# First attention of a two-layer mixture kernel: chunk ends and output gates move from GpSimd to VectorE, and five batch steps in place of six stand beside the scatter of rows

## The reference

```python
# gated linear attention, 4 heads, DK 128, DV 32, chunks of 64 tokens
gk = jax.nn.log_sigmoid(x @ Wgk1 @ Wgk2 + bgk2) / 16
G = jnp.cumsum(gc, axis=-2)                      # within a chunk
qg, k_intra = qc * jnp.exp(G) * scale, kc * jnp.exp(-G)
g_last = jnp.exp(G[..., -1, :])                  # the chunk ends
def step(S, inp):                                # over the 4 chunks
    o = oi_ + jnp.einsum('bhck,bhkv->bhcv', qg_, S)
    S = S * gl_[..., :, None] + jnp.einsum('bhck,bhcv->bhkv', kg_, v_)
o = o * jax.lax.rsqrt(jnp.mean(o * o, -1) + EPS) * gnw
o = o * (g * jax.nn.sigmoid(g))                  # the output gates
s = o @ Wo
# beside it, from the same normed x: 8 experts, each token to 2 of them
g = silu(experts(xn)); x = x + s * g
```

## Time and profile before

| | us |
|---|---|
| median of 3 runs | 1236.32 |
| the three runs | 1230.03, 1236.32, 1247.06 |
| the profiled execution: time | 1231.64 |
| the profiled execution: span of the core | 1229.8 |
| its mean granted clock of TensorE | 0.816 of full speed |
| busy PE, PEld, DVE, ACT, POOL | 870.0, 652.9, 657.1, 632.8, 442.0 |

### The profile page before, as it was taken

One profiled execution on the slowest core, in us unless ns is written; L12 is line 12 of the kernel. 1 busy time (PEld: TensorE's weight loads), 2 busy tenths in 40 slices (PEclk: granted clock), 3 DMA queues, 4 the chain that ended last, 5 costly groups with the idle time before them and its releaser, 6 DMA issues.

```text
span 1229.8 us, 23628 instructions
## 1 busy us (share of the span) xinstructions
PE 870.0 (71%) x8916; PEld 652.9 (53%) x8916; DVE 657.1 (53%) x1132; ACT 632.8 (51%) x1102; POOL 442.0 (36%) x470
## 2 busy tenths in 40 slices
PE   5644777989898986078883204989999999998510
PEld 4432566878787865054551002556766766666410
DVE  7762445655555422677567002766676566763345
ACT  5442346565756431444441002668788678886522
POOL 3077351213232345000002772003454445454535
PEclk9866768988899998575796556989999899998755
DMA  9411111010101121600001311120111011110052
GB/s 326 164 54 54 42 48 29 19 28 27 28 28 28 39 59 33 157 0 1 1 1 38 134 52 35 53 70 19 36 32 32 27 36 32 32 36 19 16 147 68
DMA packets 62366, 63.92 MB, mean 52 GB/s; under 512 B 7378, under 2 KB 52322, under 8 KB 62132
## 3 DMA queue, kind: packets, MB, share of 16 engines
q1 hardware_dynamic: 53300, 43.99, 12.2%
q0 software_dynamic: 8960, 18.43, 4.6%
HBM read 31.84 MB, written 30.55 MB: 51 GB/s over the span
## 4 chain that ended last, share of the span: by engine, by line
PE 41%; ACT 18%; issue 13%; DVE 13%; another core or an unknown queue 9%; POOL 3%; DMA 2%; SPq 0%; POOLq 0%; ACTq 0%; DVEq 0%
PE bank L427 5%; PE bank L642 4%; ACT L790 4%; PE bank L579 3%; PE bank L581 3%; POOL ys L1701 2%; PE bank L593 2%; PE bank L580 2%; ACT arena L1097 2%; PE bank L695 2%; PE bank L707 2%; PE bank L668 2%; PE bank L455 2%; PE bank L688 1%
## 5 line engine op out<-in xcount | busy, mean ns | idle before, releaser
L1701 POOL DMA_INDIRECT ys<-arena x152 | 151.9, 999 | 188.2 <-DVE arena L1450 84.8
L1097 ACT ACTIVATE arena<-bank 128x512 f32<-128x512 f32 x192 | 101.7, 596 | 109.0 <-remote 67.5
L1685 POOL DMA_INDIRECT xs<-arena x128 | 128.6, 1005 | 76.9 <-DVE arena L1291 39.3
L1571 DVE TENSOR_REDUCE arena<-bank 128x2 bf16<-128x512 f32 (+1 forms) x192 | 119.8, 681 | 61.3 <-remote 43.6
L579 PE MATMUL bank<-arena 128*128 128x128 bf16 x608 | 135.2, 230 | 10.9 <-DVE arena L1431 10.0
L581 PE MATMUL bank<-arena 128*128 128x128 bf16 x608 | 134.9, 230 | 0.0
L580 PE MATMUL bank<-arena 128*128 128x128 bf16 x608 | 132.3, 225 | 0.8 <-issue 0.7
L790 ACT ACT_TABLE_LOAD x71 | 91.1, 1283 | 1.2
L427 PE MATMUL bank<-arena 128*128 128x256 f32 x256 | 70.9, 438 | 19.7 <-DVE arena L1337 17.7
L1741 POOL TENSOR_TENSOR arena<-arena 128x1024 f32<-128x1024 f32 x20 | 46.9, 2343 | 94.3 <-ACT arena L1007 94.3
L1440 DVE SCALAR_TENSOR_TENSOR arena<-arena,bank 128x512 f32<-128x512 f32 x36 | 24.8, 689 | 97.4 <-ACT arena L969 80.4
(11 more groups left out here) (212 smaller groups left out, 2106.8 us busy)
## 6 DMA issues: line engine op xcount, KB each, us to landing
xs<-arena SPq DMA_DIRECT2D x19, 516.0 KB, 9.1
arena<-xs SPq DMA_DIRECT2D x38, 258.0 KB, 2.8
arena<-ys SPq DMA_DIRECT2D x32, 256.0 KB, 5.3
arena<-in_MF SPq DMA_DIRECT2D x8, 512.0 KB
ys<-arena POOLq DMA_INDIRECT x152
arena<-in_x SPq DMA_DIRECT2D x8, 256.0 KB, 5.5
arena<-in_W SPq DMA_DIRECT2D x8, 256.0 KB
xs<-arena POOLq DMA_INDIRECT x128
```

The costliest lines, as they stand in the source:

```text
L1097: act(PT[kt_][:, i, gs[0]:gs[0] + len(gs), :], bank_of["s2", b, n, i][:, :].rearrange("p (g q) -> p g q", q=w), ACT.Exp, scale=8 ** -0.5). ...
L1571: red(negM[b % 2][:, u, 32 * i + gs[0]:32 * i + gs[0] + len(gs)], kv_, op=ALU.max, negate=True).then_inc(m_max.sem, 1)
L1685: eng.indirect_dma_start(xs[l][:, :], bass.IndirectOffsetOnAxis(ap=slot_i[l][:, m:m + 1], axis=0), xrow[:, t, :], None).then_inc(rows_move ...
L1701: eng.indirect_dma_start(ys[l][:, :], bass.IndirectOffsetOnAxis(ap=yid[g % 4][:, j:j + 1], axis=0), y[:, 128 * j:128 * j + 128], None).the ...
```

## The change

The two pieces leave GpSimd's list and stand in VectorE's: the copy of the chunk ends in `scaled`, just before the first bank of queries is scaled, and the product with the gates in `gated`, just before the two multiplies that use it. The semaphores stay the same. The scatter is cut in fifths, each ahead of one of the attention's steps 1 to 5; the pieces of W1 are dealt out anew; step 6 and all that follow stand beside groups of experts, 14 steps beside groups 0 to 13.

```diff
-OUTPUTS_EARLY = 7
+OUTPUTS_EARLY = 6
@@ walk
-            for t in range(1, 7):
-                do["scatter"](0, t - 1, 6)
+            for t in range(1, 6):
+                do["scatter"](0, t - 1, 5)
                 if t == 1:
                     do["set_later"]()
                 for part in range(3):
                     do["gla"](t, part)
-                for c in range(8 * (t - 1) // 6, 8 * t // 6):
+                for c in range(8 * (t - 1) // 5, 8 * t // 5):
                     do["w1"](c)
             do["ffn0_begin"]()
             for g in range(19):
                 for part in range(3):
                     do["ffn0"](g, part)
-                    if 7 + g < 20:
-                        do["gla"](7 + g, part)
+                    if 6 + g < 20:
+                        do["gla"](6 + g, part)
@@ vector
+            def chunk_ends(b):
+                P5 = bufP.rearrange("p (h n i) -> p n h i", h=4, n=4)
+                if b >= 4:
+                    eng.wait_ge(*state.at(b - 4))
+                cp(ends[b % 4], P5[:, 0:3, :, 63:64].rearrange("p n h o -> p n (h o)")).then_inc(p_ends.sem, 1)
+
             def scaled(b):
                     eng.wait_ge(*qk.at(b, n))
                     if n == 0:
                         eng.wait_ge(*pn.at(b))
+                        chunk_ends(b)
                         if b >= 3:
                             eng.wait_ge(*o_mm.at(b - 3))
             def gated(b):
+                eng.wait_ge(*o_rs.at(b))
+                if b == 0:
+                    eng.wait_ge(*silu_done.at(NG - 1))
+                tt(ors[b % 2], ors[b % 2], s_all[:, 2 * b:2 * b + 2, :].rearrange("p t d -> p (t d)"), ALU.mult).then_inc(o_gate.sem, 1)
                 eng.wait_ge(*o_gate.at(b))
@@ gpsimd
-            def chunk_ends(b):
-                P5 = bufP.rearrange("p (h n i) -> p n h i", h=4, n=4)
-                eng.wait_ge(*pn.at(b, 0))
-                if b >= 4:
-                    eng.wait_ge(*state.at(b - 4))
-                eng.tensor_copy(ends[b % 4], P5[:, 0:3, :, 63:64].rearrange("p n h o -> p n (h o)")).then_inc(p_ends.sem, 1)
-
-            def output_gates(b):
-                eng.wait_ge(*o_rs.at(b))
-                if b == 0:
-                    eng.wait_ge(*silu_done.at(NG - 1))
-                tt(ors[b % 2], ors[b % 2], s_all[:, 2 * b:2 * b + 2, :].rearrange("p t d -> p (t d)"), ALU.mult).then_inc(o_gate.sem, 1)
-
-            def gla(t, part):
-                if part == 0 and 0 <= t - 4 < NB:
-                    output_gates(t - 4)
-                if part == 1 and 0 <= t - 1 < NB:
-                    chunk_ends(t - 1)
```

More of the change, by code:

```diff
@@ L1769, in nothing @@
                 pass
-            walk({"setup": setup, "set_gates": nothing, "set_later": nothing, "norm": norm, "gla": gla, "route": route, "scatter": scatter, "w1": nothing,
+            walk({"setup": setup, "set_gates": nothing, "set_later": nothing, "norm": norm, "gla": nothing, "route": route, "scatter": scatter, "w1": nothing,
                   "ffn0_begin": begin0, "ffn0": experts0, "mha_begin": nothing, "join": join, "last_join": last_join, "mha1": nothing, "mha2": nothing,
```

## The result

The changed kernel took 1256.2 us (median of 4 runs, 1251.6 to 1259.4) beside 1240.2 us for the kernel before (4 runs, 1230.0 to 1247.1): 1.0139 of it, 95% interval 1.0089 to 1.0189. By the 2% that count here that is no change, but it is 16 us slower, on the upper side of the forecast of 1237 us and outside its range (1225 to 1250).

The account below looks back on a forecast made before the run. GpSimd's unbroken indirect DMAs were taken to slow TensorE in attention steps 3 to 5; +7.6 - 4.9 + 0 = +2.7 us gave 1234.3 on the profiled time, 1239.0 on the median, forecast 1237, range 1225 to 1250.

Parts of the forecast that it names:

- The burst is what holds TensorE, and pauses let it go: First attention, steps 3 to 5: TensorE and signals crawl while GpSimd issues indirect DMAs, more so the longer without pause.
- The move makes the burst unbroken, 146.7 us at its end: Layer 1's 64 scatters: without copies and gate products they run through, ending at 146.7 us where it was 172.3.
- Up to 122.0 all is as before: First attention up to 122.0 us, within step 3: same course as in the old kernel, since the burst held it.
- Term one: Attention steps 3 to 5 beside and after the burst: step 5 ends at 187.4 instead of 179.8, +7.6 us.
- (a): Step 3, lower bound: 1.2 matmuls a us, remaining matmuls through by the release at 148.5; step 3 ends at 151.0.
- (b): Step 3, upper bound: one matmul in 2.8 us, release at 148.9, then 6.9 us; step 3 ends at 155.8.
- The case that I kept for the range: Step 3 at the second layer's pace and with its late release of 8.2 us: step 3 ends at 161.8.
- The expert rows can be loaded at about 158: Start of layer 1's experts: rows loadable some 11 us after the burst's end, earlier than anything needs them.
- the rival without a crawl: Steps 3 to 5 cost 17 each, expert rows bound at 160.5 instead of 179.8: -24.2 us, about 1212; chance 0.11.
- Five chunks, -4.9 us: Border between attention and experts: one step alone less, one combined step more, one group alone less: -17.0 + 20.9 - 8.8.
- VectorE's new work, 0: Gate product (0.42 us) and chunk copy (0.20) on VectorE: hidden behind waits, 0, bounds -1 and +10 us.
- The slower one: Late signals stop ScalarE or VectorE in step 3's first half; step 5 ends at 205.9, +21.2 us, about 1258; chance 0.08.

Follow-up runs that it names:

- lots: Changed kernel with GpSimd's layer 1 scatters split into 15 groups, each waiting for the attention step beside it: 0.9917 on a slow chip, 1.0106 on a fast one.
- five chunks alone: Kernel before with five attention chunks beside the scatter instead of six, copies and gate products still on GpSimd: 1.0003 on a slow chip, 1.0078 on a fast one.
- move alone: Changed kernel with six chunks beside the scatter instead of five: 1.0169 of the kernel before on a slow chip, 0.9918 on a fast one.
- four in flight: Changed kernel with each scatter, both layers, also waiting for the landing of the fourth before it: 1.0025 of the kernel before on both kinds of chip.

## Why the prediction was wrong, step by step

- *The burst is what holds TensorE, and pauses let it go.* Right, for the stalling chips. With the scatter off GpSimd the third step ends at 103.3 us; with lots or with the products in the queue it ends at 119 to 141, unbroken at 161 to 164.
- *The move makes the burst unbroken, 146.7 us at its end.* Right: 149.3, 1.4 of the 2.6 us being a later first scatter (63.11, before 61.69).
- *"Up to 122.0 all is as before."* Wrong, and the first part of the failure. Step 2 ended at 115.5 in place of 95.4, and at 122.0 TensorE was at the scores (L455) and had the 56 small matmuls of `outputs` still before it. Why is open. The copies of the chunk ends did not hold GpSimd back in the kernel before. Its timeline shows no idle time before the copy in step 2, and the next scatter follows at once:

```profile
89.80 0.95 POOL L1685 DMA_INDIRECT xs<-arena  x1 [0.30 <-issue]
90.75 0.21 POOL L1715 COPY arena<-arena 128x12 f32<-128x12 f32 x1
91.13 0.98 POOL L1685 DMA_INDIRECT xs<-arena  x1 [0.17 <-issue]
```

Up to 119.8 the old burst was thus as unbroken as the new one. On stalling chips, in one profiled execution each, step 2 ends at 95.4 (before), 104.8 (five chunks alone), 108.8 (move alone), 115.5 (changed) and 140.7 (four in flight). The move and the five chunks could each have a part in this, or it is spread between executions. The pieces of W1, which I priced at nothing, show no wait there: ScalarE splits both of step 2's from 94.43 without idle time.
- *Term one, +7.6 us, what TensorE does meanwhile.* This is the term that was mis-sized and the step that failed: +16.2. Step 3 ended at 163.4 where I had 153.4. Of these 10.0 us the later end of the burst makes 2.6. TensorE's late release makes 3.0: 4.9 us after the burst, where the middle of (a) and (b) has 2.0. What was left of step 3 at the release makes 4.4: scores, states, outputs, queries and keys took 9.1 us, where that middle has 4.7. The rate of the matmuls is not the fault. The measured one, 0.5 a us, lies between those of (a) and (b), and (b) alone would have given 155.8. The fault is that step 3 had hardly begun: its parts are handed from engine to engine, and the signals came only behind the burst. In the three kernels with an unbroken burst step 3 ends 14.0 to 15.5 us after the end of the last scatter, wherever step 2 ended (108.8, 115.5 or 140.7). The case that I kept for the range, 161.8 for step 3 and so 195.8 for step 5, is within 0.2 us of the 196.0 measured. That is luck: its release is 3.3 us too late, its burst ends 2.6 too soon, its rest of the step is 2.2 too short and its steps 4 and 5 are 1.4 too long.
- *The expert rows can be loaded at about 158.* Wrong, and without cost here. SyncE's first load of rows starts at 181.76, 32 us behind the last scatter and nearly where it was (182.12). In SyncE's queue the loads of W1 stand ahead of it; piece 7 waits until piece 5 is split, which VectorE does from 179.54. So the 10.8 us in the rival without a crawl were no price of the rows: on the quiet chip the load starts 1.8 us after the scatter (150.5 to 152.36).
- *Steps 4 and 5 at 17.0 each.* Right: 15.4 and 17.2.
- *Five chunks, -4.9 us.* On the recorded pair the part from step 5's end to the last expert output gave -0.4: the eleven combined steps 6 to 16 take 23.5 us more than the ten before, not 20.9, and the rest up to the last output is 7.0 shorter, not 8.8. On stalling chips the ratios with five against six are 1.0003 to 1 with GpSimd's products and 1.0139 to 1.0169 without, and the last output moves by -0.4 and -5.7 us. So its size on such a chip stays open between these two. Added up for the profiled execution: 1234.3 as forecast, 8.6 of excess in term one, 4.5 in this one and 5.8 in the second layer, for which the sum had no term, give 1253.2, and 1253.3 was measured. On a quiet chip it has the other sign, +11.8 us (423.3 to 435.1), because there the experts wait for the landed scatter; the sum had no term for that.
- *VectorE's new work, 0.* Right, at 0.42 and 0.17 us with 2.07 us of idle time left behind it. Nor did the moved copies hold up a scatter by their own length: the scatters beside the copies at 78.98 and 97.86 (at 78.59 and 97.57) take 0.96 us like the rest. The running sums do, as in the earlier trace rows: beside the one of 116.73 a scatter takes 2.66.
- *The rivals.* The slower one named the mechanism that came: late signals stop VectorE and ScalarE already ahead of step 3's second half. It got 0.08. It had step 5 end at 205.9, and it ended at 196.0, because TensorE was free 4.9 us after the burst and not 8.2, and 9.1 us of the step were left and not 17. The case without a crawl is what a quiet chip does: TensorE idle for the rows of the experts and a first expert at 155 us where I had worked out 160.5. But there the kernel before doesn't crawl either, so nothing of the 24 us is gained. The Trainium skill ("SBUF — State Buffer", Who interferes with whom) has TensorE wait for no one. In this stretch the quiet chips' traces agree, with 285 and 393 matmuls in 40 us in the kernels before and changed. The 2.53 us of idle time ahead of a 0.27 us matmul on the recorded chip do not. The section speaks of SBUF's ports, and no run here shows by what TensorE is held.

What stays open: by what path the indirect DMAs hold up TensorE's issue and the engines' signals, why some chips do it and others don't, why step 2 was late, and what shortened the second layer of the kernel with four in flight.

## What to carry to other kernels

Ask of each instruction taken out of a queue what it had waited for: a small product that waits for another engine can be the brake that keeps a long burst of DMAs from running ahead, and taking it off costs more than its own time can save. In a stretch where signals come late, don't count instructions at a rate: count as still to do everything that has to be handed from one engine to another (here nearly the whole of step 3, 14 to 15.5 us behind the last scatter). And find what each part waits for at its start: chunks placed ahead of a scatter's landing were nearly free on one kind of chip, and worth nothing behind it.

## What was unexpected of the hardware

- The six chips of the experiments fell into two kinds for one and the same kernel, 1078 to 1079 and 1226 to 1237 us, and a change can have opposite signs on them: the move alone is 0.992 on the one and 1.017 on the other, the scatters in lots with five chunks 1.011 and 0.992.
- On the one kind a run of indirect DMAs on GpSimd, 1.27 us from start to start and at most four in flight, brings TensorE to one matmul in 2.0 us on the mean and in 2.8 us at the worst, and holds signals to VectorE and ScalarE back for 25 to 38 us; 64 plain DMAs from SyncE for the same bytes do nothing of the kind.
- TensorE runs freely again within 5.3 us of the end of the last scatter in layer 1 and within 10 in layer 2.
